# Second graph layer: half of each gathered row copied into PSUM by ScalarE, and three early gathers instead of eight and five

## The reference, cut to what matters

```python
def gatv2(x, src, dst, Ws, bs, Wd, bd, attn):
    H, D = attn.shape
    fs = (x @ Ws + bs).reshape(-1, H, D)
    fd = (x @ Wd + bd).reshape(-1, H, D)
    e = jax.nn.leaky_relu(fs[src] + fd[dst], 0.2)
    logits = jnp.einsum('ehd,hd->eh', e, attn)
    ...
x = x + _L0_gnn_ref(_layernorm(x), src, dst, ...)   # layer 1, layer norm, layer 2
```

## Time and profile before

| | us |
|---|---|
| median of 3 runs | 3865.47 (3865.23 to 3866.54) |
| the profiled execution | 3864.15 |
| its span, first to last instruction | 3862.4 |
| PE busy | 3497.6 (91%) |
| DVE busy | 2321.7 (60%) |
| ACT busy | 1426.7 (37%) |
| POOL busy | 1325.8 (34%) |

### The profile page before, as it was taken

How to read it: one execution, slowest core, us unless ns; L and a number is a source line. 1 busy time by engine, 2 the same in 40 slices (tenths; PEclk the granted TensorE clock), 3 DMA queues, 4 the chain that set the end, 5 groups by cost and what they waited for, 6 DMA issues and landing times. The chain is left out here.

```text
span 3862.4 us, 72697 instructions
## 1 busy us (share of the span) xinstructions
PE 3497.6 (91%) x18522; PEld 2214.2 (57%) x18523; DVE 2321.7 (60%) x8037; ACT 1426.7 (37%) x4300; POOL 1325.8 (34%) x1316
## 2 busy tenths in 40 slices
PE   6979999779999898999767779998999996999998
PEld 4657777545555466777656654544557673444443
DVE  5359999978888757999989967511151233111111
ACT  0037777658888412222377743310010100000000
POOL 0036666547777006777566640000000000111111
PEclk9989999889999999999989999999999997999999
DMA  3258888748888428999677740015400008611245
GB/s 125 76 182 293 293 291 293 255 154 296 292 294 295 145 74 289 321 322 324 222 262 218 217 154 1 1 49 192 188 5 25 29 1 306 203 31 34 73 152 167
DMA packets 185752, 689.60 MB, mean 179 GB/s; under 512 B 32114, under 2 KB 54562, under 8 KB 185258
## 3 DMA queue, kind: packets, MB, share of 16 engines
q0 software_dynamic: 104624, 484.82, 38.6%
q1 hardware_dynamic: 80826, 203.07, 15.4%
q10 hardware_dynamic: 192, 0.25, 0.0%
HBM read 921.95 MB, written 40.51 MB: 249 GB/s over the span
## 5 line engine op out<-in xcount | busy, mean ns | idle before, releaser
L724 PE MATMUL l_psZ<-X,ident 128*128 128x396 f32 (+3 forms) x2656 | 807.1, 426 | 0.0
L667 POOL DMA_INDIRECT X<-fs,near_src x648 | 612.0, 944 | 318.6 <-DVE l_psZ L681 309.2
L724 PEld LDWEIGHTS l_psZ<-X,ident 128*128 128x128 f32 x2656 | 497.0, 190 | 185.4 <-issue 1.5
L721 PE MATMUL l_psZ<-fd,spread 128*128 x1328 | 450.4, 420 | 35.2 <-issue 35.1
L1010 PE MATMUL a_psO<-X,a_sel 128*128 128x396 f32 (+1 forms) x1328 | 458.4, 504 | 3.3 <-DVE X L964 3.2
L993 ACT ACTIVATE X<-X,L 128x99 f32<-128x99 f32 x1328 | 373.8, 365 | 85.7 <-DMA X<-fs,pair_src 83.8
L948 POOL DMA_INDIRECT X<-fs,pair_src x324 | 347.3, 1072 | 100.5 <-issue 97.6
L1010 PEld LDWEIGHTS a_psO<-X,a_sel 128*128 128x128 f32 x1328 | 236.9, 190 | 224.4 <-issue 71.8
L687 DVE SCALAR_TENSOR_TENSOR l_zr<-l_psZ,attn 128x99 f32<-128x99 f32 x1660 | 324.0, 255 | 0.2 <-issue 0.2
L694 DVE SCALAR_TENSOR_TENSOR l_zr<-l_psZ,attn 128x772 f32<-128x772 f32 x332 | 315.9, 952 | 0.0
L651 ACT ACTIVATE l_zr<-l_zr 128x99 f32<-128x99 f32 x996 | 270.2, 273 | 106.2 <-DVE l_zr L692 106.2
(11 more groups left out here) (516 smaller groups left out, 5271.9 us busy)
## 6 DMA issues: line engine op xcount, KB each, us to landing
ew_w<-in_L_ffn_w SPq DMA_DIRECT2D x276, 1152.0 KB
dsts<-near_rows SPq DMA_DIRECT2D x166, 128.0 KB
room<-in_L_ffn_w SPq DMA_DIRECT2D x8, 2304.0 KB
hw_w<-in_L_ffn_w SPq DMA_DIRECT2D x24, 576.0 KB
ew_b1t<-in_L_ffn_b SPq DMA_DIRECT2D x46, 288.0 KB
X<-fs,near_src POOLq DMA_INDIRECT x664, 5.3
H<-in_L_ffn_b SPq DMA_DIRECT2D x46, 192.0 KB
X<-in_x SPq DMA_DIRECT2D x2, 3456.0 KB
```

What stands on the lines that cost most here:

```text
L667: nc.gpsimd.indirect_dma_start(out=g[:, n % RING, :], out_offset=None, in_=fs, in_offset=bass.IndirectOffsetOnAxis(ap=R.near_src[:, n:n + ...
L721: nc.tensor.matmul(psZ[k][:, a, 0:half], spread[:, j // 4, k, :], R.fd[:, ds(b, 1), lo:hi].squeeze(1), start=True, stop=True)
L724: last = nc.tensor.matmul(psZ[k][:, a, 0:hi - lo], R.ident[:], g[:, j, lo:hi], start=False, stop=True, skip_group_check=True)
```

## The change

The second layer's `logits` is replaced by a new function, `logits_copied`; the first layer keeps `logits`. The number of gathers that are issued in the projections becomes 3 (`BEGUN`) in both layers; the others up to the eighth are issued at the start of the logits by POOL.

In `logits_copied` ACT copies the second half of each gathered row (386 columns) into the second bank of `psZ[k]`, when the row has landed and DVE has reduced the visit 4 before. PE waits for that copy, spreads `fd[dst]` into the first half with start=True, spreads it into the second half with start=False, so that it is added to what ACT has put there, and adds the first half of the gathered row by the identity (386 columns). The 193-column product and DVE's `join` are gone, and with them `s_z`: POOL waits for PE's `s_mm` of the visit 8 before. ACT's two operations for a batch are dealt between its copies. Before the loop PE makes four products with start=True into the second banks, and ACT waits for them (`s_begun`).

```diff
+BEGUN = 3
...
         @block.gpsimd                                  # in project, layer 1
-            first_gathers(nc, R, table, width, 0, GATHERED)
+            first_gathers(nc, R, table, width, 0, BEGUN)
...
+def logits_copied(nc, R, name, fs, heads, begun):
...
+        @block.scalar
+        def _(act):
+            act.sem_inc(s_spread, 3)
+            act.sem_inc(s_away, 3)
+            act.sem_inc(s_mm, 8)
+
+            def distances(t, s, i):
+                act.wait_ge(s_d[s], i * 16 + 16)
+                act.wait_ge(s_spread, t + 1)
+                nc.scalar.activation(away[:, s], dsts[:, s, :], ACT.Abs, bias=R.minus_near[:]).then_inc(s_away, 1)
+
+            def one_hots(t, s):
+                act.wait_ge(s_mm, t * 4 + 4)
+                act.wait_ge(s_away, t + 3)
+                nc.scalar.activation(spread[:, s].rearrange("p k e -> p (k e)"), away[:, s], ACT.Relu, scale=-1.0, bias=one[:]).then_inc(s_spread, 1)
+
+            def copy(n, j, i):
+                act.wait_ge(s_g[j], i * 16 + 16)
+                act.wait_ge(s_part, n + 1)
+                nc.scalar.copy(psZ[j % 4][:, 1, 0:half], g[:, j, half:width]).then_inc(s_copied, 1)
+
+            act.wait_ge(s_begun, 1)
+            with act.Fori(0, PAIRS) as i:
+                for s in range(2):
+                    t = i * 2 + s + 1
+                    copy(i * 8 + s * 4, s * 4, i)
+                    distances(t, 1 - s, i + s)
+                    copy(i * 8 + s * 4 + 1, s * 4 + 1, i)
+                    copy(i * 8 + s * 4 + 2, s * 4 + 2, i)
+                    one_hots(t, 1 - s)
+                    copy(i * 8 + s * 4 + 3, s * 4 + 3, i)
+            for j in range(4):
+                copy(BATCHES * 4 - 4 + j, j, PAIRS)
+
+        @block.gpsimd
+        def _(pool):
+            first_gathers(nc, R, fs, width, begun, RING)
+            for n in range(RING, NEAR_VISITS):
+                pool.wait_ge(s_mm, n - RING + 9)
+                nc.gpsimd.indirect_dma_start(
+                    out=g[:, n % RING, :], out_offset=None, in_=fs,
+                    in_offset=bass.IndirectOffsetOnAxis(ap=R.near_src[:, n:n + 1], axis=0)).then_inc(s_g[n % RING], 16)
+
+        @block.vector
+        def _(dve):
...
+            def reduce(n, j):
+                k = j % 4
+                dve.wait_ge(s_mm, n + 9)
...
+                    last = nc.vector.scalar_tensor_tensor(out=zr[:, k, :].rearrange("p (a e) -> p a e", a=2), in0=psZ[k][:, :, 0:half], scalar=0.0,
+                                                          in1=at[:].rearrange("p (a e) -> p a e", a=2), op0=ALU.max, op1=ALU.mult, accum_out=R.L[:, 0, ds(n, 1)])
+                last.then_inc(s_part, 1)
...
+        @block.tensor
+        def _(pe):
+            def visit(n, j, t):
+                k = j % 4
+                b = pe.value_load(R.near_block[0:1, ds(n, 1)], min_val=0, max_val=NEAR_BLOCKS - 1)
+                if k == 0:
+                    pe.wait_ge(s_spread, t + 3)
+                pe.wait_ge(s_copied, n + 1)
+                rows = R.fd[:, ds(b, 1), :].squeeze(1)
+                nc.tensor.matmul(psZ[k][:, 0, 0:half], spread[:, j // 4, k, :], rows[:, 0:half], start=True, stop=True)
+                nc.tensor.matmul(psZ[k][:, 1, 0:half], spread[:, j // 4, k, :], rows[:, half:width], start=False, stop=True, skip_group_check=True)
+                nc.tensor.matmul(psZ[k][:, 0, 0:half], R.ident[:], g[:, j, 0:half], start=False, stop=True, skip_group_check=True).then_inc(s_mm, 1)
+
+            for k in range(4):
+                last = nc.tensor.matmul(psZ[k][:, 1, 0:half], spread[:, 0, k, :], R.fd[:, 0, half:width], start=True, stop=True)
+            last.then_inc(s_begun, 1)
...
         @block.gpsimd                                  # in finish_project, layer 2
-            first_gathers(nc, R, table, width, 0, KD * D // width)
+            first_gathers(nc, R, table, width, 0, BEGUN)
...
-                        logits(nc, R, "l1", fs, heads, GATHERED)
+                        logits(nc, R, "l1", fs, heads, BEGUN)
...
-                        logits(nc, R, "l2", fs, heads, KD * D // width)
+                        logits_copied(nc, R, "l2", fs, heads, BEGUN)
```

More of the change, by code:

```diff
@@ L731, in _, with load @@
                 visit(BATCHES * 4 - 4 + j, j, PAIRS, BATCHES - 1)
+def logits_copied(nc, R, name, fs, heads, begun):
+    hd, he = D // heads, head_width(heads)
+    width = heads * he
+    half = width // 2
+    RING = GATHERED
+    PAIRS = BATCHES // 2
+    with Scope(nc, name) as c:
+        at, away, one, spread = R.at, R.away, R.one, R.spread
+        g, s_g = gathered(R, width), R.s_near
+        dsts, s_d = R.dsts, R.s_dsts
+        zr = c.sb("zr", [P, 4, width])
+        psZ = [c.ps(f"psZ{k}", [P, 2, BANK]) for k in range(4)]
+        s_v, s_away, s_spread, s_copied, s_mm, s_part = (c.sem(x) for x in ("v", "away", "spread", "copied", "mm", "part"))
+        s_begun = c.sem("begun")
+        block = c.enter_context(nc.Block())
+        @block.sync
+        def _(sp):
+            def load(t, s):
+                sp.wait_ge(s_away, t + 1)
+                sp.dma_start(dsts[:, s, :], R.near_rows[0:NEAR_VISITS].rearrange("(t k) p -> t (k p)", k=4)[ds(t, 1), :].squeeze(0).partition_broadcast(P)).then_inc(s_d[s], 16)
+            with sp.Fori(0, PAIRS - 1) as i:
+                for s in range(2):
+                    load(i * 2 + s + 2, s)
+            load(BATCHES - 1, 0)
+        @block.scalar
[17 more added lines that the diff above has]
+            with act.Fori(0, PAIRS) as i:
+                for s in range(2):
+                    t = i * 2 + s + 1
[17 more added lines that the diff above has]
+        def _(dve):
+            chain = Chain(dve, s_v)
+            dve.sem_inc(s_part, 4)
+            chain(nc.vector.memset(R.L[:, :, NEAR_VISITS:NEAR_LIST], 0.0))
+            def reduce(n, j):
+                k = j % 4
+                dve.wait_ge(s_mm, n + 9)
+                if heads > 1:
+                    for h in range(heads):
+                        lo, hi = h * he, (h + 1) * he
+                        last = nc.vector.scalar_tensor_tensor(out=zr[:, k, lo:hi], in0=psZ[k][:, lo // half, lo % half:lo % half + he], scalar=0.0, in1=at[:, lo:hi],
+                                                              op0=ALU.max, op1=ALU.mult, accum_out=R.L[:, h, ds(n, 1)])
+                else:
+                    last = nc.vector.scalar_tensor_tensor(out=zr[:, k, :].rearrange("p (a e) -> p a e", a=2), in0=psZ[k][:, :, 0:half], scalar=0.0,
+                                                          in1=at[:].rearrange("p (a e) -> p a e", a=2), op0=ALU.max, op1=ALU.mult, accum_out=R.L[:, 0, ds(n, 1)])
+                last.then_inc(s_part, 1)
+            with dve.Fori(0, PAIRS) as i:
+                for j in range(8):
+                    reduce(i * 8 + j, j)
+            for j in range(4):
+                reduce(BATCHES * 4 - 4 + j, j)
+            dve.wait_ge(s_part, NEAR_VISITS + 4)
+        @block.tensor
[13 more added lines that the diff above has]
+            last.then_inc(s_begun, 1)
+            with pe.Fori(0, PAIRS) as i:
+                for j in range(8):
+                    visit(i * 8 + j, j, i * 2 + j // 4)
+            for j in range(4):
+                visit(BATCHES * 4 - 4 + j, j, BATCHES - 1)
```

## The result

| | us |
|---|---|
| median before, beside it | 3865.35 (3864.72 to 3866.54, 4 runs) |
| median after | 3832.21 (3830.39 to 3835.04, 4 runs) |
| ratio | 0.9915, 95% interval 0.9897 to 0.9932 |
| predicted | 3835.7 (3829 to 3850) |
| span of the profiled execution after | 3833.3 |

A forecast was written before the change was run, and what follows sets the result against it. PE bounds the layer-2 logits at 1.33 us per visit; afterwards POOL's gather issue does at 1.25. Gains of 22.8 (layer-2 stage), 5.0 and 2.0 (early gathers) make 29.8 us: 3835.7 us, range 3829 to 3850.

The forecast's parts named there:

- PE, 1.01 us: Layer-2 logits: without the two 193-column instructions, PE's period per visit falls from 1.33 to 1.01 us.
- DVE, 1.0 us: Layer-2 logits: with the join gone, DVE needs 0.88 us per visit, 1.0 allowed with bookkeeping, against 1.33 before.
- ACT, 0.50 us for a copy: Layer-2 logits: ACT's new 386-column copy from SBUF to PSUM takes 0.50 us, 0.86 us of ACT work per visit.
- Rival D: Layer-2 loop: ACT's program order costs up to 0.72 us per batch; at half its bound, 30 us, time is 3865; chance 0.04.
- POOL, 1.25 us per gather: Layer-2 logits: POOL never waits for a slot and sets the pace, one gather every 1.25 us per visit.
- POOL's pauses, 4.7 us: Layer-2 logits: three gaps of 2.8 us between gathers, no longer caught up, cost 1.56 us each, 4.7 us.
- The DMA engines: Layer-2 loop: 342 GB/s asked for at 1.25 us per visit; 374 GB/s seen earlier, 1.14 us per visit, so not the bound.
- The layer-2 stage: Layer-2 logits: the stage ends at 423.6 us in place of 446.4, a gain of 22.8 us.
- Fewer early gathers: Projections: five fewer gathers in layer 1 save 5.0 us, two fewer in layer 2 save 2.0; layer-1 logits lose nothing.
- Rival B: Projections: early gathers bring nothing, so only layer 2's loop gains and the time is 3842.7 us; chance 0.07.
- The sum: Whole kernel: 22.8 + 5.0 + 2.0 = 29.8 us gained, giving 3835.7 us; no later stage takes from these.
- Rival C: Layer-2 loop: PE's rests drop its clock to 1.2 GHz, 1.97 us per visit; half the time so, 3930 us; chance 0.05.

The follow-up runs named there:

- e6: Changed kernel with two more 126-column identity products per layer-2 visit on PE, into columns nobody reads: 3899.17 us, 65.8 more than c0.
- e5: Changed kernel with one more 126-column identity product per layer-2 visit on PE, into columns nobody reads: 3831.04 us, ratio to the kernel before 0.9917.
- e4b: Changed kernel with ScalarE copying the whole 772-column row into both banks and PE's identity product gone, beside a 3865 us kernel before: 3831.62 us, ratio 0.9915.
- e3: Changed kernel with layer-2 loop gathers fetching 386 of 772 columns, number of gathers unchanged: 3829.51 us, ratio to the kernel before 0.9908.
- c0: The changed kernel run once more, unaltered, as comparison for the runs beside it: 3833.34 us against 3865.48 before, ratio 0.9921.
- e1b: Kernel before with three early gathers in both projections and nothing else, second run: 3856.64 us against 3865.57, ratio 0.9979.
- 4035 us group: The group of e1, e2, e4 and e7 (first runs), in which the unchanged kernel before took 4035.24 us instead of 3865; they are compared with it alone.
- e4: Changed kernel with ScalarE copying the whole row and PE's identity product gone; first run, in the 4035 us group: 4054.36 us, ratio to the kernel before 1.0043.
- e7: Changed kernel with layer 1 using the copying logits too: 4137.45 us, ratio 1.0256, in the 4035 us group; run again, 3819.17 us, ratio 0.9878.
- e1: Kernel before with three early gathers in both projections and nothing else; first run, in the 4035 us group: 4032.23 us, ratio 0.9992.

## Why the prediction was right, point by point

- **PE, 1.01 us.** Right: at the stage's end, where its work is lined up, PE's last products start 1872.93 - 1871.92 = 1.01 us apart; by e6 it is 1.03. POOL's pace covers it in e5. The sign that was to go with it, PE busy for about 80%, did not come: the profile shows 93%, modelled ends included.
- **DVE, 1.0 us.** Not contradicted: its last reductions start at 1872.77 and 1873.78, 1.01 us apart, but each starts 0.04 us after PE's products end, so this step is PE's, and DVE's own is at most that. No run moved DVE's load in layer 2; that it doesn't set the pace rests on its idle time, 95.8 us before 332 reductions.
- **ACT, 0.50 us for a copy.** Right: 482 ns, the same as the 384-column copy out of PSUM. The order of its program cost nothing, and e4b, with copies of 772 columns, shows that even the fuller ScalarE fits under 1.25 us (318.95 us for 297 visits, 1.07 each). Rival D is out where the kernel before takes 3865 us.
- **POOL, 1.25 us per gather.** Right, and it is the bound: e3, e4b and e5 each move another load, of the DMA engines, of PE and ScalarE, of PE, and the stage stays within 2 us of c0's.
- **POOL's pauses, 4.7 us.** Wrong, and this is the one step of the sum that failed. The prediction let each pause cost its full 1.56 us; there are none. Before and in e1b and e6, where POOL waits for its slots, they come every 106 gathers. In c0, e3 and e5, where its wait is over when it arrives, they don't. That a pause would still be there without its cover was taken over from the profile before and had no row of a POOL that doesn't wait behind it.
- **The DMA engines.** Right: 342 GB/s were asked for and moved, with a share of 0.96 and a landing of 5.5 us. The catch-up stretch of the earlier trace rows was the better guide than the share: a share of 0.94 did not mean 6% of room at most. The estimate of 2.9 us for a landing, by the formula of the Trainium skill (DMA: Bandwidth & Descriptors, "Anatomy of one DMA — SWDGE (gpsimd) path"), is not met by the traces: whole rows land after 5.5 us, and even half the bytes after 3.7.
- **The layer-2 stage.** Predicted 423.6, measured 418.0. The last gather starts 1867.14 - 1456.72 = 410.4 us into the stage in place of 415.4, which is the pauses (4.7) and a step of 1.2498 in place of 1.2506, and the way from there to the end is 7.6 us in place of 8.2.
- **Fewer early gathers.** Right: from POOL's first early gather to the next stage's first instruction it is 12.3 us in place of 17.2 in layer 1 (4.9, predicted 5.0), and 11.9 in place of 13.8 in layer 2 (2.0, predicted 2.0). The layer-1 stage gave nothing back: 506.3 against 505.9 by the measure of the table. Rival B is out.
- **The sum.** The three places give 28.4 + 4.9 + 2.0 = 35.2 us, 5.4 more than predicted, and the medians show 33.1 and 32.1. That no later stage takes from the gain was not quite so: the experts' stage takes 617.5 to 619.3 us in all eight profiles with the copying logits outside the 4035 us group, and 616.1 and 616.0 before and in e1b. Some 2 us go there. The cause was not tried. That 3835.7 came within 3.5 us of the measured 3832.2 is in part luck: the sum was 5.4 us too small in the three places, and the loss behind them made up a part of that.
- **Rival C, PE's clock.** It did not come in the changed kernel: a granted clock of 1.00 (2.4 GHz) through the loop, with PE busy for 93% of it. But the mechanism is real in this kernel's neighbours. With PE's load per visit made lighter, e4's loop runs at 0.50 (1.2 GHz) in both groups, and e7's layer-1 loop in the 4035 us group goes to and fro between 0.51 and 0.99. The alternation is what the Trainium skill describes for a PE that rests between groups of products (TensorE: Matmul & The Clock Gate, "A second HAM failure mode: psum-queue depth-cycling"): e7's trace in the 4035 us group agrees with it, e4's steady 0.50 does not. The price of a visit at half clock, put at 1.97 us (2 x 0.97 + 0.04 is 1.98), is near e7's 1.98 us for products of 396 columns.

## What to carry to other kernels

When the bound of a loop is relieved, look in the profile of before for a stretch in which the next engine was late and caught up: its step there is the new pace, and what the transfers moved there is what they can do. A pause that an engine shows while it waits need not be there when it no longer waits, so it is a term with two ends, not a fixed cost. And a version that leans on transfers or on a PE at part load should be measured more than once, beside the kernel before each time: e7 is 1.2% faster than it in one group and 2.6% slower in another.

## What the runs showed of the hardware that was not expected

- The same program, the kernel before, took 3865 us in three groups of runs and 4035 in one, with the runs of a group within 0.3% of each other, and with nearly the whole difference in the four stages that gather rows. In e1 against e1b, by the measure of the table, the layer-1 logits take 544 us against 506, the layer-2 logits 520 against 448, the layer-1 sums 502 against 462, the layer-2 sums 347 against 323; the layer-2 loop moved 276 GB/s where 322 were moved before. The cause stays open.
- PE at a granted clock of 0.50 for over 450 us on end (e4b), with no cost: its two products kept it busy for 1.00 us per visit (297.71 us for 297), and that fitted under 1.25.
- POOL's pause of about 1.6 us at every 106th gather, only where it waits for its slots; e5 and e6 show it absent and present with one product between them.
- A copy by ScalarE from SBUF into PSUM took what one out of PSUM took: 482 ns for 386 columns, 480 for 384. One of 772 columns into PSUM took 798 ns (e4b), one of 768 within SBUF 835.
